# A graph layer with routed experts: x1 fetched by token instead of queued, and a rewritten routing stage

## The reference

```
m = layernorm(x)                               # over the 256 columns
H = m.astype(float16);  v = edge_weight.astype(float16)
x = x + segment_sum(H[dst] * v[:, None], src)  # fp16 sums, N segments
h = layernorm(x)
logits = h @ gate_w + gate_b;  probs = softmax(logits);  idx = argmax(probs)
pos = rank of the token among those of its expert, in token order
kept = pos < C                                 # C = ceil(1.25 * 50000 / 8)
y = relu(h @ w1[idx] + b1[idx]) @ w2[idx] + b2[idx]     # 256 -> 1024 -> 256
x = x + nan_to_num(y * probs[idx] * kept)
```

## Time and profile before

| | |
|---|---|
| median of 3 runs | 3526.37 us |
| the profiled execution | 3569.06 us, span 3567.3 us |
| edge stage | 0 to 712 us |
| routing stage | 713.8 to 1465 us; first addition (L661) 723.3, the 49th 1413.5 |
| expert stage | 1465 to 3567 us |
| busy share of the span | PE 80%, DVE 63%, POOL 48%, ACT 43% |

### The profile page before, as it was taken

One profiled execution on the slowest core, in us unless ns is written; L12 is line 12 of the kernel. 1 busy time (PEld: TensorE's weight loads), 2 busy tenths in 40 slices (PEclk: granted clock), 3 DMA queues, 4 the chain that ended last, 5 costly groups with the idle time before them and its releaser, 6 DMA issues.

```text
span 3567.3 us, 60077 instructions
## 1 busy us (share of the span) xinstructions
PE 2846.6 (80%) x18806; PEld 2603.9 (73%) x18807; DVE 2245.0 (63%) x5836; ACT 1539.7 (43%) x2638; POOL 1724.4 (48%) x1183
## 2 busy tenths in 40 slices
PE   4553434067677777499999999999999999999998
PEld 3443433067676667399898999888999989998987
DVE  5645555076566566377666677676677776667666
ACT  2322222044444444255444555454455545554443
POOL 4788887635555566333434333343433343334323
PEclk8666666555555555699999999999999999999999
DMA  8544444388787776311211211121211121111111
GB/s 313 153 89 77 87 78 86 29 269 252 249 259 248 228 240 207 115 48 56 66 57 44 72 48 52 49 67 57 67 48 47 56 67 47 48 51 49 42 47 37
DMA packets 306007, 374.74 MB, mean 105 GB/s; under 512 B 34887, under 2 KB 266340, under 8 KB 302608
## 3 DMA queue, kind: packets, MB, share of 16 engines
q1 hardware_dynamic: 224608, 202.49, 19.3%
q0 software_dynamic: 77728, 145.22, 14.9%
q10 hardware_dynamic: 3600, 26.22, 1.8%
HBM read 185.42 MB, written 196.46 MB: 107 GB/s over the span
## 4 chain that ended last, share of the span: by engine, by line
PE 53%; DVE 4%; issue 1%; DVEq 0%; DMA 0%; SPq 0%; ACT 0%; POOL 0%; POOLq 0%; ACTq 0%
PE u_Y L1181 27%; PE u_H L1170 23%; PE u_T L1153 3%; DVE y L1110 1%; DVE yo L1129 1%; DVE yo L1126 1%; DVE y L1115 0%; DVE hn L1078 0%; DVE low L1120 0%; DVE hlo L1098 0%; DVE yo L1124 0%; DMA slots<-blank 0%; DMA u_pay<-slots 0%; DVE scales L1073 0%; DVEq L1078 0%
## 5 line engine op out<-in xcount | busy, mean ns | idle before, releaser
L1010 POOL DMA_INDIRECT out_x<-yo,u_token x348 | 668.5, 1921 | 1261.4 <-DVE yo L1131 1179.5
L1181 PE MATMUL u_Y<-whi,hhi 128*128 128x256 f32 x2784 | 784.2, 282 | 1.5 <-DVE hlo L1098 1.5
L1181 PE MATMUL u_Y<-wlo,hhi 128*128 128x256 f32 x2784 | 775.4, 279 | 0.0
L1181 PE MATMUL u_Y<-whi,hlo 128*128 128x256 f32 x2784 | 774.8, 278 | 0.0
L1046 ACT ACTIVATE hm<-u_H,b1e 128x512 f32<-128x512 f32 (+1 forms) x736 | 487.9, 663 | 639.8 <-PE u_H L1170 627.0
L539 POOL DMA_INDIRECT slots<-pay,slot_i x392 | 415.3, 1059 | 325.5 <-DVE slot_i L748 210.3
L1170 PE MATMUL u_H<-xhi,whi 128*128 128x512 f32 (+1 forms) x1472 | 563.6, 383 | 8.0 <-issue 5.5
L1170 PE MATMUL u_H<-xhi,wlo 128*128 128x512 f32 (+1 forms) x1472 | 562.2, 382 | 0.0
L1170 PE MATMUL u_H<-xlo,whi 128*128 128x512 f32 (+1 forms) x1472 | 560.2, 381 | 0.0
L1181 PEld LDWEIGHTS u_Y<-whi,hhi 128*128 128x128 f32 x2784 | 528.4, 190 | 1.7 <-DVE hlo L1098 1.7
L1181 PEld LDWEIGHTS u_Y<-wlo,hhi 128*128 128x128 f32 x2784 | 528.8, 190 | 0.0
(11 more groups left out here) (137 smaller groups left out, 3747.9 us busy)
## 6 DMA issues: line engine op xcount, KB each, us to landing
xt<-in_x SPq DMA_DIRECT2D x49, 1024.0 KB
out_x<-pay SPq DMA_DIRECT2D x49, 1024.0 KB
u_pay<-slots SPq DMA_DIRECT2D x93, 534.0 KB, 3.8
agg<-zeros ACTq DMA_DIRECT2D x25, 1024.0 KB
at<-agg SPq DMA_DIRECT2D x49, 512.0 KB
raw<-in_L_ffn_w POOLq DMA_DIRECT2D x14, 1024.0 KB
src_row<-in_src SPq DMA_DIRECT2D x25, 512.0 KB
slots<-blank SPq DMA_DIRECT2D x8, 801.0 KB, 5.1
```

The source lines that it names most:

```text
L1010: pool.indirect_dma_start(out=out[:, :], out_offset=bass.IndirectOffsetOnAxis(ap=token[:, s:s + 1], axis=0), in_=yo[:, s, :], in_offset=No ...
L1181: last = pe.matmul(ps_Y[:, s, 0:D], a[:, f, rows], w2_at(w, buf, f), start=(f == 0 and j == 0), stop=(f == KF - 1 and j == 2))
```

## The change

In the constants the record shrinks to 11 numbers (44 bytes): mean, 1/std, token number, 8 logits. The ring of the routing stage becomes eight, that of `at` four.

Routing, rewritten:
- tokens stand as p*8+g, so that a partition's eight rows are contiguous in memory;
- PE carries `agg` into PSUM: eight fp16 matmuls with the identity a step (`aggregate`), one step ahead; DVE then adds `ps_A` to `x1` in place;
- the gate's bias is put in by one fp32 matmul with the identity; `ps_T` has two banks in place of four; ranks take 23 small fp16 matmuls, and stand ahead of the last gate part;
- token numbers are made by ACT; several small DVE operations go (`lg`, `kept_hot`, copies of mean and token);
- SP stores x1 three steps after it was computed;
- the first expert's weights are split by POOL, ahead of its first scatters.

Experts: SP loads records alone, into one buffer, after the unit before has been normalised. POOL fetches the rows of x1 from `out` by token (`gather`, four indirect DMAs) for the unit two ahead, into one buffer; ACT copies them to one of four kept copies (`hold`) for the final addition; DVE copies the records to `own`.

```diff
-MEAN, RSTD, TOKEN, LOGIT = 256, 257, 258, 259
-RING = 4
+MEAN, RSTD, TOKEN, LOGIT = 0, 1, 2, 3
+RING = 8
+AGGS = 4
...
+            def aggregate(i, r):
+                s = RING * i + r
+                pe.wait_ge(agg_loaded[r % AGGS], 16 * ((RING // AGGS) * i + r // AGGS + 1))
+                if not (isinstance(i, int) and s == 0):
+                    pe.wait_ge(x1_ready, s)
+                for g in range(G):
+                    last = pe.matmul(ps_A[:, g, :], ident16[:], at[:, r % AGGS, g, :], start=True, stop=True)
+                last.then_inc(agg_up, 1)
...
-                pe.matmul(ranks[:, 0:G, :], before[:], hot[:, q], start=True, stop=False, skip_group_check=True)
                 for g in range(G):
-                    last = pe.matmul(ranks[:, g + 1:G + 1, :], ones[:],
-                                     hot[:, q, g, :].unsqueeze(1).broadcast_to([P, G - g, E]),
+                    pe.matmul(ranks[:, 0:g + 1, :], before[:],
+                              hot[:, q, g, :].unsqueeze(1).broadcast_to([P, g + 1, E]),
+                              start=(g == 0), stop=False, skip_group_check=True)
+                for g in range(G - 1):
+                    pe.matmul(ranks[:, g + 1:G, :], upto[:],
+                              hot[:, q, g, :].unsqueeze(1).broadcast_to([P, G - 1 - g, E]),
+                              start=False, stop=False, skip_group_check=True)
+                for g in range(G):
+                    last = pe.matmul(ranks[:, G, :], ones[:], hot[:, q, g, :],
                                      start=False, stop=(g == G - 1), skip_group_check=True)
...
+                if k == 0:
+                    if not (isinstance(i, int) and s < 1):
+                        pe.wait_ge(hot_ready, s)
+                    pe.matmul(logits, ident[:], gb[:].unsqueeze(1).broadcast_to([P, G, E]),
+                              start=True, stop=False, skip_group_check=True)
...
+                    aggregate(*((i, r + 1) if r + 1 < RING else (i + 1, 0)))
+                turn(i, r, 0)
+                turn(i, r, 1)
+                gate(i, r, 0)
+                turn(i, r, 2)
+                gate(i, r, 1)
+                turn(i, r, 3)
+                gate(i, r, 2)
+                if not (isinstance(i, int) and s == 0):
+                    rank(*before_of(i, r, 1))
+                gate(i, r, 3)
...
-                v.tensor_tensor(pay[:, r, :, 0:D], xt[:, q], at[:, q], ALU.add).then_inc(x1_ready, 1)
+                v.wait_ge(agg_up, s + 1)
+                v.wait_ge(x_loaded[r], 16 * (i + 1))
+                v.tensor_tensor(x1[:, r], ps_A[:], x1[:, r], ALU.add).then_inc(x1_ready, 1)
...
# run_experts, SP
                 def unit(u, row):
-                    sp.wait_ge(y_ready, u + (1 - RING + SEED["y_ready"]))
+                    sp.wait_ge(hn_ready, u + SEED["hn_ready"])
...
# POOL
+            def gather(u):
+                pool.wait_ge(rec_loaded, 16 * (u + 1))
+                pool.nop(nofuse=True)
+                pool.wait_ge(kept, u + SEED["kept"])
+                pool.nop(nofuse=True)
+                for s in range(SUB):
+                    pool.indirect_dma_start(
+                        out=x1[:, s, :], out_offset=None, in_=out[:, :],
+                        in_offset=bass.IndirectOffsetOnAxis(ap=rec[:, s, TOKEN:TOKEN + 1].bitcast(I32), axis=0),
+                        bounds_check=N - 1, oob_is_err=False,
+                    ).then_inc(gathered, 16)
+            gather(0)
+            gather(1)
             load_weights(1)
...
                 def unit(u, subs):
+                    gather(u + LEAD)
                     pool.wait_ge(y_ready, u + 1 + SEED["y_ready"])
...
# ACT
+            def hold(u):
+                act.wait_ge(gathered, 16 * SUB * (u + 1))
+                if not isinstance(u, int):
+                    act.wait_ge(y_ready, u + (1 - KEEP + SEED["y_ready"]))
+                    act.nop(nofuse=True)
+                act.activation(keep[:, u % KEEP], x1[:], ACT.Copy).then_inc(kept, 1)
...
-                    act.activation(ex[:], pay[:, u % RING, :, LOGIT:LOGIT + E], ACT.Exp).then_inc(ex_ready, 1)
+                    act.activation(ex[:], own[:, u % 2, :, LOGIT:LOGIT + E], ACT.Exp).then_inc(ex_ready, 1)
+                    hold(u + 1)
                     for f in range(KF):
...
# DVE
-                v.wait_ge(pay_loaded, 16 * (u + 1))
-                v.tensor_copy(scales[:], pay[:, u % RING, :, MEAN:RSTD + 1]).then_inc(scales_ready, 1)
+                v.wait_ge(gathered, 16 * SUB * (u + 1))
+                v.tensor_copy(own[:, u % 2], rec[:])
...
-                    v.tensor_tensor(yo[:, used], yo[:, used], pay[:, u % RING, used, 0:D], ALU.add).then_inc(y_ready, 1)
+                    v.tensor_tensor(yo[:, used], yo[:, used], keep[:, u % KEEP, used], ALU.add).then_inc(y_ready, 1)
```

More of the change, by code:

```diff
@@ L507, in _, with body @@
[L507 to L513, removed]
+            def body(i, r):
+                if not (isinstance(i, int) and RING * i + r < LEAD):
+                    store(*before_of(i, r, LEAD))
+                load(i, r)
+            steps(sp, S, RING, body)
@@ L558, in body, with normalise @@
                 act.nop(nofuse=True)
+                def normalise(k):
+                    for g in range(k * G // BANKS, (k + 1) * G // BANKS):
+                        last = act.activation(h[:, q, g, :], x1[:, r, g, :], ACT.Identity,
+                                              bias=shift[:, q, g:g + 1], scale=rec[:, r, g, RSTD:RSTD + 1])
+                    last.then_inc(h_ready, 1)
                 def copy(k):
@@ L565, in copy @@
                     part = slice(k * PER_BANK, (k + 1) * PER_BANK)
[L566 to L570, removed]
-                                              bias=shift[:, q, g:g + 1], scale=pay[:, r, g, RSTD:RSTD + 1])
-                    last.then_inc(h_ready, 1)
-                    if k:
-                        copy(k - 1)
-                copy(BANKS - 1)
+                    act.activation(hT[:, part, :], ps_T[:, k % 2], ACT.Copy).then_inc(hT_ready, 1)
+                normalise(0)
+                normalise(1)
+                copy(0)
+                normalise(2)
+                copy(1)
+                if not (isinstance(i, int) and s == LAST):
+                    deviation(*((i, r + 1) if r + 1 < RING else (i + 1, 0)))
+                normalise(3)
+                copy(2)
+                copy(3)
+            deviation(0, 0)
             steps(act, S, RING, body)
@@ L751, in body @@
+                v.scalar_tensor_tensor(out=slot_i[:, r, :], in0=where[:], scalar=float(E * QUEUE), in1=full[:],
+                                       op0=ALU.add, op1=ALU.add).then_inc(slot_ready, 1)
             def body(i, r):
                 s = RING * i + r
-                a = Count(s * PER_A + SET)
-                statistics(i, r, a)
-                scales(i, r, a)
+                add(i, r)
+                statistics(i, r)
+                if not (isinstance(i, int) and s < 2):
+                    slot(*before_of(i, r, 2))
@@ L1054, in _ @@
             act.wait_ge(b1_ready, 1)
+            hold(0)
             upper(0)
```

423 lines of the change are left out of this document (225 added, 198 removed).

## The result

The changed kernel takes 3954.95 us (median of 4, 3950.51 to 3958.23), against 3533.62 us for the kernel before: a ratio of 1.119, 95% interval 1.116 to 1.123. The forecast was 3750 in a range of 3600 to 3900: the right side, but 205 us short, and outside the range. Its profiled execution has a span of 3956.5 us, 389 more than before.

What follows compares the result with a forecast made beforehand. PE was taken to bound both routing (with late signals added) and expert stages. Profiled 3569 - 54 (routing and its start) + 280 (experts) = 3795; the profiled execution stood 42.7 above the median, so 3750, range 3600 to 3900.

Steps and rivals of the forecast that it cites:

- where the experts lose: Expert stage: `hold` waits for fetched rows, making PE 4.8 us late about every second unit; 2.1 a unit, 139 us.
- the term of the low clock: Expert stage: PE at clock 0.50 after gaps, 1.7 us each, up to +45 us; little of it taken.
- +280: Expert stage's total loss in us: 139 steady units, 105 changes of expert, 16 halves, 20 start; bounds 145 and 360.
- what I expect to vanish is the late signals: Routing: "remote" waits of ACT and DVE, 3.8 us a step, vanish as scatter traffic falls 96%; stage -50 us.
- Rival C: Routing: late signals stay, coming with any indirect DMA; 16.9 us a step, +122 us, kernel 3924; chance 0.12.
- PE's 13.1 and one join: Routing step: 13.1 us of PE work bound it; the chain from rank to turn beside gate 3 and `aggregate` makes 13.4.
- the start: Routing stage's start: first expert's weight split moves from DVE to POOL; -4 us, bounds -7 to +12.
- Rival A: Routing: PE's clock rises once fed, POOL's scatters bound the step at 11 us; -167 us, kernel 3635; chance 0.15.
- Rival B: Expert stage: the second scatter is no longer blocked; loss 160 instead of 280 us, kernel 3632; chance 0.15.
- D: Expert stage: `hold` doesn't stop ACT, so only the start's +20 us is lost; kernel 3496; chance 0.11.

Runs made afterwards that it cites:

- the late copy: Changed kernel with ACT's `hold` moved behind the eight relus and the upper part of the unit; 3686.22 us, ratio 1.043.
- the padding: Changed kernel with `hold` behind the relus, plus an unused 2240 bytes per partition ahead of `hn`, restoring the addresses of before; 3608.71 us, ratio 1.050.
- the mended kernel: Changed kernel with square root late, first split on DVE, `hold` behind relus, 2240 unused bytes; 3417.99 us, ratio 0.994; with late signals 3653.75, 1.026.

## Why the prediction was wrong

**Right: where the experts lose.** The times on the path of a unit were forecast within half a us: rows there at T+28.5 (measured 28.2), relu at T+30.3 (30.1). PE was late by 3.74 us instead of 4.8, every second unit as forecast; it came to its third block at T+26.4 and not at T+25.5, 0.67 us of it because its passes were slower (see the addresses).

**Mis-sized, the term of the low clock.** The prediction had the earlier trace rows before it, priced a gap at 1.7 us, and took little of up to 45 us, since most gaps are 4 or less. Gaps of 3.7 us were enough, and one costs 3.1 or 1.9 by turns: 89 us over the stage. By the late copy, what `hold` stopped is 181 us of gaps and 89 us at the lower clock, 271 in all. The late copy leaves 83 - 57 = 26 us of other gaps, and 2081 - 2021 = 60 us of slower passes (most of them by the next point): 181 + 89 + 26 + 60 = 356, the whole difference. The prediction's +280 was gaps alone; they measure 207. So the gaps were put 73 too high, and the clock's 89 and the passes' 60 were left out.

**Missing, the addresses.** No step of the prediction asked whether buffers that move change the speed of PE's reads. They did, by 0.67 us a unit. With the padding PE is busy 47 to 48 us less and waits 4 to 10 us more, so 37 to 43 us come back; the other 13 of the 60 us aren't explained. The rest of +357, which `hold` doesn't make, is 43 to 46 us at the start, the halves and the changes of expert (2120.6 and 2124.2 in the mended traces against 2078 to 2080).

**Wrong, the step "what I expect to vanish is the late signals".** It read a coincidence in time (the waits end as the scatter's records land) as one of bytes. The records shrank by 96% and the waits stayed; one scatter in place of eight took them away. Rival C, "they come with any indirect DMA", was nearer to the cause, with 0.12 of the chance, but had too much follow from it, 16.9 us a step: the ring hid most of them.

**Missing, the ring.** The prediction put the step at PE's 13.1 and one join. PE's sum was about right (580.5 us busy in 48 steps, 12.1 each; with the clock at 0.55 not all of it was at the lower level). It looked at what each engine does and at the chain from rank to turn, but not at what stands in ACT's program between two normalisations: a wait for the next step's statistics. Added up, from 1.9 of `aggregate` to gate 3, that chain is longer than PE's work. On a chip without late signals it costs 3.7 us a step (14.24 in the changed kernel, 10.50 in the mended one on the same chip; 180 us). The two also differ in the split's place, the late copy and the padding, but none of these is in a step, and a trace with the ring, the padding and the late copy has 14.23.

**Wrong in sign, the start.** -4, with bounds of -7 to +12; measured +6.4 from the edge stage's last scatter on, and 5.6 ahead of it, which the prediction put at nothing. POOL's work was priced at 3 us of disturbance; it stopped DVE for its full length, and by the split's place alone the first addition comes 7.5 us later.

**The rivals.** Rival A (clock up when fed): hardly in the changed kernel, where the ring starves PE and the clock was 0.55 (forecast 0.50), but in the mended one, with a step of 10.50 us and the clock at 0.65; the rival's 11 was nearly that. The sentence of the Trainium skill ("TensorE: Matmul & The Clock Gate", Part 4) by which transposes don't count as busy spoke against it; in the mended kernel 16 of some 80 passes a step are transposes, 3.2 of the 10.2 us that PE is busy, and the clock rose, so a mix with transposes can reach the upper level. But the kernel before with one scatter stayed at 0.50 with PE busy 95% (499 of 524 us) and transposes a larger part of its work, so it doesn't clear them either: what lets the clock rise was not tried by itself. Rival B (the second scatter unblocked) didn't occur: 4.81 us. Nor did D (`hold` doesn't stop ACT): the rows came at 1608.3, 4.8 us after the H that had to wait for them had begun (1603.5).

## What to carry to other kernels

A wait that is moved ahead of work of the same engine has to be followed once around: add up what stands between an operation and its next instance through all engines, and compare that sum, not each engine's busy time, with the step. Where PE waits regularly, price the gap twice, for its length and for the passes at the lower clock behind it. When buffers change size, compare PE's ns per pass in a stretch without gaps before looking for any other reason.

## What the runs showed of the hardware

- PE's passes depend on where its operands lie in SBUF: with `hn` and all that is laid out behind it 2240 bytes lower, Y's passes took 118.7 instead of 113.5 ns (11.40 against 10.90 for 96), at the same granted clock of 1.00. Which tile it is was not tried.
- The late signals differ from chip to chip: 165 to 187 us of waits of `hT` in the routing stage of the kernel before and its variants with eight scatters in the two groups on chip 15, none on chips 11 and 5, with the same program (3535 and 3556 against 3437 and 3438 us). What in the chip differs is open, and so is by what path scattered rows delay PE's signals.
- Gaps of 3.7 us on PE, one every second unit, were followed by 6.8 and 3.4 us at a granted clock of 0.50 by turns, and cost 3.1 and 1.9 us besides their length.
- Two DVE operations of 0.17 us each took 3.54 and 8.78 us beside POOL's cast and subtraction of 128x4096 numbers (3.59 and 8.80 us).
